# Attention kernel: output transposes of 36 columns through a strided identity, placed behind the value projection; ternary weights made in the last unit of the first pass

## The reference

```python
# layer 0
q = ln(latents); x = latents + mha(q, q)            # self-attention, 16 heads of 8
x = x + mha(ln(x), ln(tokens))                      # cross-attention over 1500 tokens
x = x + moe(ln(x))                                  # 8 experts, top 2, width 512
# layer 1
def bit_quant(W):
    gamma = mean(abs(W))
    return W + (clip(round(W / (gamma + 1e-5)), -1, 1) * gamma - W)
q = ln(x) @ bit_quant(Wq).T + bq                    # Wk, Wv, Wo likewise ternary
x = x + mha_core(q, k(context), v(context)) @ bit_quant(Wo).T + bo
```

## Time and profile before

| | us |
|---|---|
| median of 3 runs | 633.04 (632.65 to 633.94) |
| the profiled execution's own time | 633.05 |
| its span, first to last instruction | 631.3 |
| PE busy | 542.5 (86%) |
| DVE busy | 389.0 (62%) |
| ACT busy | 326.4 (52%) |
| POOL busy | 199.1 (32%) |

### The profile page before, as it was taken

How to read it: one execution, slowest core, us unless ns; L and a number is a source line. 1 busy time by engine, 2 the same in 40 slices (tenths; PEclk the granted TensorE clock), 3 DMA queues, 4 the chain that set the end, 5 groups by cost and what they waited for, 6 DMA issues and landing times.

```text
span 631.3 us, 16157 instructions
## 1 busy us (share of the span) xinstructions
PE 542.5 (86%) x6582; PEld 386.4 (61%) x6582; DVE 389.0 (62%) x974; ACT 326.4 (52%) x495; POOL 199.1 (32%) x190
## 2 busy tenths in 40 slices
PE   0699838799999999979968989378999999999996
PEld 0587515566666767747736767145666766767774
DVE  5668479677777776776234211578777677676720
ACT  1265214456767677635733333225666666666572
POOL 2553214647594854400025100224041240330000
PEclk9899769889999999979987999778999999999997
DMA  5010621634554435412200731026537437353300
GB/s 155 34 51 1 164 76 44 166 75 128 136 130 117 130 77 145 93 50 57 100 1 3 177 108 60 25 69 153 132 91 185 119 86 178 86 144 84 72 3 16
DMA packets 36987, 58.66 MB, mean 93 GB/s; under 512 B 16308, under 2 KB 20524, under 8 KB 36916
## 3 DMA queue, kind: packets, MB, share of 16 engines
q1 hardware_dynamic: 36916, 57.66, 36.1%
HBM read 17.81 MB, written 0.23 MB: 29 GB/s over the span
## 4 chain that ended last, share of the span: by engine, by line
PE 54%; issue 23%; DVE 11%; DMA 5%; POOL 3%; ACT 2%; SPq 2%; DVEq 0%; POOLq 0%; ACTq 0%
PE SM L1209 11%; PE PO L1224 11%; PE ST L1181 7%; PE MI L1123 6%; PE MI L1133 6%; DVE mxp L824 5%; PE MI L1157 2%; PE MI L1112 2%; DMA cx<-in_ctx 2%; PE SM L1296 2%; DMA qst<-mrow 1%; ACT ksplit L598 1%; PE SM L1157 1%; DVE cstat L796 1%; SPq L361 1%
## 5 line engine op out<-in xcount | busy, mean ns | idle before, releaser
L824 DVE TENSOR_REDUCE mxp<-SM 112x1 f32<-112x500 f32 x364 | 237.5, 674 | 92.0 <-PE SM L1209 91.2
L626 ACT ACTIVATE PT<-ST 128x896 f32<-128x896 f32 x192 | 171.3, 912 | 57.7 <-PE ST L1181 57.5
L1209 PE MATMUL SM<-kst,qst 96*112 96x500 bf16 x364 | 141.5, 403 | 16.8 <-DVE mxp L824 12.5
L1181 PEld LDWEIGHTS ST<-qst,kst 98*128 98x128 bf16 x1536 | 94.8, 100 | 37.2 <-issue 13.6
L1181 PE MATMUL ST<-qst,kst 98*128 98x112 bf16 x1536 | 108.9, 215 | 1.8 <-DMA qst<-mrow 1.8
L500 POOL TENSOR_TENSOR kr<-kf,ksplit 128x500 f32<-128x500 f32 x48 | 54.3, 1134 | 149.3 <-ACT ksplit L598 149.3
L1224 PE MATMUL PO<-PT,vaug 125*32 125x112 f32 x3072 | 98.0, 266 | 2.1 <-ACT PT L626 1.5
L1224 PEld LDWEIGHTS PO<-PT,vaug 125*32 125x32 f32 x3072 | 71.7, 111 | 24.9 <-issue 16.2
L1209 PEld LDWEIGHTS SM<-kst,qst 96*112 96x112 bf16 x364 | 46.9, 131 | 48.8 <-DVE mxp L824 31.8
L610 ACT ACTIVATE vaug<-MI 125x512 f32<-125x512 f32 x48 | 28.7, 598 | 77.4 <-PE MI L1133 77.4
L505 POOL TENSOR_TENSOR ksplit<-kr,ksplit 128x500 bf16<-128x500 f32 x48 | 54.6, 1138 | 41.7 <-DVE ksplit L819 41.7
(11 more groups left out here) (131 smaller groups left out, 544.0 us busy)
## 6 DMA issues: line engine op xcount, KB each, us to landing
kst<-ksplit SPq DMA_DIRECT2D x192, 187.5 KB, 3.8
cx<-in_ctx SPq DMA_DIRECT2D x8, 750.0 KB
xT<-in_ctxT SPq DMA_DIRECT2D x8, 750.0 KB, 5.1
moe<-in_w1T SPq DMA_DIRECT2D x8, 256.0 KB, 2.9
moe<-in_w2T SPq DMA_DIRECT2D x8, 256.0 KB, 3.0
qall<-qsplit SPq DMA_DIRECT2D x12, 112.0 KB, 2.3
qst<-qall SPq DMA_DIRECT2D x56, 21.0 KB, 1.9
watt<-in_watt SPq DMA_DIRECT2D x1, 768.0 KB, 5.3
```

Of the source, the lines that this page charges most:

```text
L626: nc.scalar.activation(PT[:, k % PTB], ST[:, k % 2, :, 0:4 * PC], ACT.Exp, scale=SCALE).then_inc(exp_done, 1)
L824: nc.vector.tensor_reduce(mxp[:, j // 3, j % 3:j % 3 + 1], tile_bank(j, banks), AX.X, ALU.max).then_inc(sm_red, 1)
L1181: last = mm(ST[:, k % 2, cc, PC * p:PC * (p + 1)], kst[n.par][:, 4 * half + p, at:at + 128], qst[n.par][:, 4 * half + p], start=True, stop ...
L1209: mm(tile_bank(j, banks), qst[n.par][0:SROWS, j // 3], kst[n.par][0:SROWS, j // 3, at:at + THIRD], start=True, stop=True).then_inc(sm_full, 1)
```

## The change

Three things change.

1. `transpose_po` sends only 36 columns of the identity through the array instead of 128: nine columns out of each group of 32, read with a stride of 32 (`rows_of[:, :, VW * hh:VW * (hh + 1)]`), and the output is packed densely. The weights stay the same, 56 columns of `po`. `normalise` reads the dense form.
2. `output_back` moves from step 3 to step 7, behind the value projection of steps 4 to 6; `normalise_unit` on DVE moves from step 3 to step 8, and `output_forth` from step 7 to step 9. The steps of the value projection stay.
3. `ternary_weights` moves from unit 5, step 6, to unit 7, step 0.

```diff
-K_STEP, BACK_STEP, V_STEP, FORTH_STEP, CTX_STEP = 0, 3, 4, 7, STEPS - 3
+K_STEP, V_STEP, BACK_STEP, FORTH_STEP, CTX_STEP = 0, 4, 7, 9, STEPS - 3
@@ normalise
-                heads = bank[0:L].rearrange("q (h x) -> q h x", x=32)
+                heads = back[0:L, 0:H * VW].rearrange("q (h x) -> q h x", x=VW)
@@ window, on DVE
-                    if k == BACK_STEP and (n + -1).exists():
+                    if k == BACK_STEP + 1 and (n + -1).exists():
                         normalise_unit(n + -1)
@@
-                    if n.s == 0 and n.c == B - 3 and k == HSTEP:
+                    if n.s == 0 and n.c == B - 1 and k == 0:
                         ternary_weights()
@@ transpose_po
+                rows_of = ident[:].rearrange("k (p x) -> k p x", x=32)
                 for half in range(2):
                     for hh in range(2):
-                        at = 256 * half + (128 - VW) * hh
-                        last = mm(bank[0:L, at:at + 128], po[:, PC * half + L * hh:PC * half + L * (hh + 1)],
-                                  ident[:], start=True, stop=True, skip_group_check=True)
+                        at = 4 * VW * (2 * half + hh)
+                        last = mm(back[0:L, at:at + 4 * VW], po[:, PC * half + L * hh:PC * half + L * (hh + 1)],
+                                  rows_of[:, :, VW * hh:VW * (hh + 1)], start=True, stop=True,
+                                  skip_group_check=True)
```

More of the change, by code:

```diff
@@ L851, in place_q, with normalise @@
                 last.then_inc(qst_ready, 1)
-            def normalise(bank, full, rden_sem, done, full_at, rden_at, par):
+            def normalise(back, full, rden_sem, done, full_at, rden_at, par):
                 dve.wait_ge(full, full_at)
-                heads = bank[0:L].rearrange("q (h x) -> q h x", x=32)
+                heads = back[0:L, 0:H * VW].rearrange("q (h x) -> q h x", x=VW)
                 nc.vector.reciprocal(rden[:], heads[:, :, DH]).then_inc(rden_sem, 1)
@@ L1149, in transpose_max, with transpose_po @@
                                     identb[0:PC, 0:PC]).then_inc(mx_full, 1)
-            def transpose_po(bank):
+            def transpose_po(back):
+                rows_of = ident[:].rearrange("k (p x) -> k p x", x=32)
                 for half in range(2):
                     for hh in range(2):
-                        at = 256 * half + (128 - VW) * hh
-                        last = mm(bank[0:L, at:at + 128], po[:, PC * half + L * hh:PC * half + L * (hh + 1)],
-                                  ident[:], start=True, stop=True, skip_group_check=True)
+                        at = 4 * VW * (2 * half + hh)
+                        last = mm(back[0:L, at:at + 4 * VW], po[:, PC * half + L * hh:PC * half + L * (hh + 1)],
+                                  rows_of[:, :, VW * hh:VW * (hh + 1)], start=True, stop=True,
+                                  skip_group_check=True)
                 return last
```

## The result

The changed kernel takes 625.86 us (median of 20 runs, 620.95 to 632.39); the kernel before, run beside it on the same chip, 634.11. The ratio is 0.9857 [0.9834, 0.9881]. It is faster, as forecast, but by 8 to 9 us instead of 19. The forecast of 614.1 and its range are missed. The profiled execution took 624.32 us. Two of the 20 runs took over 1.5% more than the fastest of them, and the ratio leaves such runs out.

What follows compares the result with a forecast made beforehand. The prediction took PE's own order to bound the kernel, held up by DVE and DMAs. Savings of 3.8 + 7.4 - 2.4 + 3.6 + 6.6 = 19.0 from 633.05 gave 614.1 us, range 608.5 to 621.0.

Steps and rivals of the forecast that it cites:

- Self-attention, -3.8: Self-attention: eight shorter transpose calls on PE's path, seven of them saving 0.54 us each, 3.8 us in all.
- One saving is lost: Self-attention: one of eight call savings of 0.54 us goes, as PE there starts only when DVE's p_sa is done.
- when the stretches shift: Whole kernel: the granted clock, below full in several stretches, can move the time by about 2 us either way.
- Units 4 and 5, and 1 to 5 of pass 1, 1.05 each: Seven units: 1.2 gained at step 3, 0.48 paid at step 7, 0.33 given back; 7.4 us in all.
- the 0.33 given back at step 8: Step 8 of a unit: 0.33 us of the moved call lies in the tile's existing wait for DVE.
- Units 1 to 3 of pass 0, +0.79 each: Step 3's gain is lost waiting for the keys' DMA; turn forth waits 0.43 and loses cover 0.36; 2.4 us lost.
- not the DMA's: Rival: the gap at t4[1] in pass 0 isn't the DMA's, so three units gain 1.05 in front; 610.9 us, chance 0.11.
- Ternary weights, -6.6: Unit 5 of pass 0: the 4.12 us wait goes, and 2.5 of the slow-clock stretch behind it; 6.6 us gained.
- Units 6 and 7, -1.8 a pass with the end: End of each pass: unit 6 gains 0.75, unit 7 about 0.5, the call at the end 0.54; 3.6 us for both.
- Pass 1's loads: Rival: the loads of pass 1 bind too, so its five units gain nothing; 619.4 us, chance 0.14.
- The transposes do not get shorter: Rival: something other than the moved columns sets 0.127 us an instruction; 20 places lose 0.54 each, 624.9 us, chance 0.10.
- strided reading is slow: Rival: reading the identity in runs of nine with stride 32 is slow for PE; slower than before, 644.5 us, chance 0.02.

Runs made afterwards that it cites:

- POOL few: The changed kernel with POOL's third part of the keys (line 505) on 8 of 500 columns, the rest left out; 622.78 us, ratio 0.9817.
- narrow only: The kernel before with the 36-column transposes alone, steps and ternary weights as before; 628.60 us, ratio 0.9902.
- small context: The changed kernel, leaving out eleven of twelve chunks of the context loaded in the units of pass 0; 618.74 us, ratio 0.9733.
- division early: The changed kernel with DVE's division at step 7, behind that step's tiles and in front of the statistics; 624.17 us, ratio 0.9855.
- keys first: The changed kernel with SP's context load behind the restacking of the keys instead of in front; 624.46 us, ratio 0.9856.
- spread: The changed kernel with the two context normalisation pieces of step 5 of self-attention put on steps 5 and 7; 620.97 us, ratio 0.9806.
- three mends: The changed kernel with spread, keys first and division early together; 620.16 us, ratio 0.9752.
- moved only: The kernel before with both turns and DVE's division at the new steps, but 128 columns and ternary weights as before; 638.86 us, ratio 1.0043.

## Why the prediction was wrong

**Self-attention, -3.8: wrong, and half of the miss.** The step that failed is "One saving is lost", the sum of seven savings of 0.54. It came to +0.97. The call itself was right (0.53 for a forecast 0.48). But what stands against the saving is more than one call:

- DVE's piece at step 5 holds PE whatever the calls take; one saving is lost there, as forecast. But the narrow calls also bring the piece forward onto POOL's line 500, and its cast takes 0.46 more. That this cast is POOL's doing rests on the times and on the same cast in pass 1, which *POOL few* frees; line 500 itself was not taken away.
- Behind the hold the granted clock falls to half. `attnT` starts at 54.34, 61.53 and 66.05 after, and at 54.23, 59.85 and 62.92 before. The first gap is 1.57 longer, of which 0.46 is the cast: 1.1. The second is 1.45 longer though a call in it is 0.48 shorter: 1.9. Together 3.0 us, nearly all that was forecast as gain. The table shows it: all six kernels with narrow calls and the piece unspread have a dip that begins between 56 and 59 us (changed, narrow only, small context, division early, keys first, POOL few). None of the six with wide calls has one that begins between 35 and 70 us, and none of the three with narrow calls and the spread piece one that begins between 35 and 64. These are single executions, but the clock of the whole span agrees over all runs of three pairs that differ in self-attention's calls alone: narrow and wide, it is 0.921 and 0.930 (*changed*), 0.927 and 0.932 (*spread*), 0.924 and 0.927 (*three mends*), over 20 runs of the changed kernel and 6 of each of the others. I had given the clock 2 us either way, "when the stretches shift", and had not tied it to shorter calls. The runs tie the dip near 58 us to narrow calls together with the unspread piece; what in them brings it they do not show. *POOL few* says that the length of the wait is not it alone, since the dip stays with a wait of 1.05.

The Trainium skill, "SBUF — State Buffer", section "Who interferes with whom", says that VectorE and GpSimd share one pair of ports under an exclusive lock, that a cast or a tensor_scalar in a two-port mode takes it, and that the second one to start blocks until the first is done. The trace agrees: 54.27 and 54.28 after, 53.70 and 53.71 before. I had read that page for another rule and not for this one.

**Rest of the clock.** At the end (+0.26 for a forecast -0.54) the call is 0.5 shorter, and the stretch runs at a clock of 0.56 instead of 0.66. But with the same code the end takes 10.4 us at 0.72 in *spread*, so this difference is not shown to be the change's. Over the runs the whole span's clock averages 0.921 after (20 runs) and 0.928 before (54 runs); a straight line through the 20 runs of the changed kernel gives about 4 us for 0.01. By that line 3 us of the miss are the clock's, wherever they fall. That is a correlation and no test. The start (+1.26 to `crstd`) differs by as much between kernels with the same code, so it is not shown to be the change's either.

**Units 4 and 5, and 1 to 5 of pass 1, 1.05 each: right in kind, too large.** Measured 0.75. Two terms of the sum were too large. The value projection came 1.05 earlier and not 1.2, as two new waits for DVE, 0.16 and 0.10, stand where the 0.51 was. And the 0.33 given back at step 8 was read off the row of the weight load (PEld) in the earlier trace rows; PE's own idle time there was 0.16, in the row shown above. With both put right the sum is 1.05 - 0.48 + 0.16 = 0.73. *Narrow only* and *moved only* split the 0.75: 0.48 for the call, 0.27 for the move. The miss is 1.5 us in pass 1 and 0.6 in pass 0.

**Units 1 to 3 of pass 0, +0.79 each: right in kind, too small in size.** Measured +0.76, +1.54 and +0.95. Both reasons were shown: *small context* and *keys first* take the wait at t4[1] away, *division early* that of the turn forth. The sum was 3.25 for a forecast 2.4. Unit 2 is longer than unit 1 by 0.78: its last key DMA was issued 0.33 later in the unit and took 8.81 us to land instead of 8.58, so PE waited 1.60 and not 1.04 at t4[1], and then 0.65 and not 0.42 for a tile's reduction. In the kernels with the same code in pass 0 the three units take 84.41 to 85.93 together. The rival "not the DMA's" is out.

**Ternary weights, -6.6: right.** Unit 5 gave 6.66 with this edit alone, the wait and the dip behind it.

**Units 6 and 7, -1.8 a pass with the end: a little too large.** 0.96 and 0.94 instead of 1.25.

**The other rivals.** Pass 1's loads do not bind: four of its five units fell by 0.75. Only unit 5 is 0.6 longer than these (24.78), as before (25.49), and in some kernels of the table it is 24.18 too. "The transposes do not get shorter" and "strided reading is slow" are out by 0.53 us a call. The section of the Trainium skill that the prediction names for this would allow a price for the lines that a run of nine touches; no run here compares it with a dense read of 36 columns. The prediction's count of hits holds for the runs that begin at column 0 of a group, with 4, 4 and 1; those that begin at column 9 have 3, 4 and 2. The other rule of the Trainium skill, a weight load of an estimated 47 ns for 56 columns, gives 0.37 us a call where the trace has 0.53.

## What to carry to other kernels

When a sum counts a wait as covered or given back, take it from the row of the engine that bounds the stretch: here the weight load's row said 0.33 and the matmul's 0.16. Look also at what the engine waits for next once a wait is gone; here 0.26 of 0.68 us came back in other places. Where a helper engine's long piece sets the pace, making the main engine's work shorter saves nothing until that piece is cut or spread (in self-attention, in one execution each, the spreading gave 3.7 us and the shorter calls alone 0.5), and it can push that piece onto another engine's work. And when a queue orders a large load in front of a small urgent one, swap them before moving work around on the engine that waits: 4.7 us in three units of the profile, though the ratio of *keys first* by itself did not fall.

## What the runs showed of the hardware

- A DVE cast of 128x500 float32 takes 0.40 us alone. It takes 1.34 when it starts within 0.1 us of POOL's subtraction of the same size, and 0.86 when it starts 0.58 ahead of the end of one; it ends 0.28 us after POOL's end in both cases. DVE's next normalisation starts 0.01 us after POOL's operation is over.
- Eight matmuls of 56 weight and 36 moved float32 columns take 0.53 us; with 128 moved columns 1.02. The 0.53 hold the reading of the moved operand in runs of nine with a stride of 32; no run reads 36 columns densely, so a small price is not excluded.
- In units 1 to 3 of pass 0 the last of six restacking DMAs takes 8.2 to 9.9 us to land when a load of 750 KB was issued ahead of them, and 3.8 to 4.1 when that load is cut to a twelfth or issued behind them; PE's matmul starts 0.09 us after the landing.
- Kernels with shorter matmuls had the lower clock. Over self-attention it was 0.92 in all six kernels with calls of 128 columns, and 0.77 to 0.88 in seven of the nine with 36; it was 0.76 in the two others, of which *three mends* had a longer dip early on. PE's busy time was 39.23 us either way without the spreading.
